# Attention and mixture-of-experts kernel: the order of TensorE's value products, scores and projection pieces within two heads

## What is computed

```python
x = x + xattn(layernorm(x), ctx)      # x: 2 x 512 x 512, ctx: 2 x 1024 x 512
x = x + ffn(layernorm(x))

# xattn: 1024 queries, 2048 keys, 16 heads of 32
q, k, v = fq_sym(q * scale), fq_sym(k), fq_sym(v)        # rounded to 255 levels
attn = softmax(einsum('bhqd,bhkd->bhqk', q, k))
attn = fq_unsigned(attn)                                 # rounded to 256 levels of the row's maximum
out = einsum('bhqk,bhkd->bhqd', attn, v) -> (1024, 512)
return out @ Wp + bp

# ffn: 8 experts; weights from x @ Wr choose the tokens' experts
h = silu(x @ Wg[e]) * (x @ Wu[e])
out = sum over e of weights[e] * (h @ Wd[e])
```

## Time and profile before

| what | value |
|---|---|
| time, median of 3 runs | 721.15 us (719.05 to 723.45) |
| the profiled execution, its own time | 722.4 us |
| its span in the trace | 720.6 us |
| TensorE busy | 617.9 us, 86% |
| VectorE busy | 567.7 us, 79% |
| ScalarE busy | 460.4 us, 64% |
| GpSimd busy | 409.7 us, 57% |
| staging of even heads (L1443) | 64 instructions, 150.2 us |
| staging halves of odd heads (L1452) | 128 instructions, 162.3 us |
| Exp (L1104) | 127 instructions, 253.2 us |

### The profile page before, as it was taken

How to read it: one execution, slowest core, us unless ns; L and a number is a source line. 1 busy time by engine, 2 the same in 40 slices (tenths; PEclk the granted TensorE clock), 3 DMA queues, 4 the chain that set the end, 5 groups by cost and what they waited for, 6 DMA issues and landing times.

```text
span 720.6 us, 16044 instructions
## 1 busy us (share of the span) xinstructions
PE 617.9 (86%) x5440; PEld 334.1 (46%) x5440; DVE 567.7 (79%) x930; ACT 460.4 (64%) x560; POOL 409.7 (57%) x457
## 2 busy tenths in 40 slices
PE   8999998666777777777768787799999999999995
PEld 4744443333534343343435355455555555555543
DVE  6998888999999999999999998793746547464430
ACT  5444459789888899898989896443534434343421
POOL 5265576655677878787877773324334453344503
PEclk9999999999999999999999997999999999999998
DMA  7877879999999999999999996258796887968724
GB/s 261 203 152 174 183 155 189 170 173 175 182 174 182 181 198 189 192 193 186 195 189 186 192 188 151 88 197 230 180 251 140 225 218 182 251 151 230 140 33 59
DMA packets 318517, 129.44 MB, mean 180 GB/s; under 512 B 293508, under 2 KB 293508, under 8 KB 318472
## 3 DMA queue, kind: packets, MB, share of 16 engines
q1 hardware_dynamic: 311296, 112.64, 72.7%
q0 software_dynamic: 7168, 16.26, 10.8%
q10 hardware_dynamic: 8, 0.01, 0.0%
HBM read 44.33 MB, written 12.06 MB: 78 GB/s over the span
## 4 chain that ended last, share of the span: by engine, by line
PE 49%; issue 11%; DMA 11%; DVE 11%; SPq 8%; ACT 5%; POOL 3%; POOLq 0%; DVEq 0%; ACTq 0%
PE psum L1724 46%; DMA work<-work 9%; DVE spare L1452 4%; ACT work L1104 4%; SPq L485 3%; SPq L483 3%; DVE spare L1443 3%; POOL work L676 1%; PE psum L1901 1%; SPq L452 1%; PE psum L2052 1%; DMA token_region<-in_L_xattn_Wkv_dram 1%; PE psum L1729 1%; POOL out_dram L858 1%; DMA work<-x_rows,slot_tok 0%
## 5 line engine op out<-in xcount | busy, mean ns | idle before, releaser
L1104 ACT ACTIVATE work<-spare,exp_bias 128x2048 uint8<-128x2048 f32 (+1 forms) x127 | 253.2, 1994 | 32.7 <-POOL exp_bias L682 21.4
L1452 DVE TENSOR_SCALAR_CACHE_REDUCE spare<-psum,q_step_now 128x1024 f32<-128x1024 f32 x128 | 162.3, 1272 | 3.4 <-PE psum L1901 3.2
L676 POOL CAST work<-work 128x2048 int16<-128x2048 uint8 x70 | 132.4, 1892 | 33.9 <-DMA work<-work 25.5
L1443 DVE TENSOR_SCALAR_CACHE_REDUCE spare<-psum,q_step_now 128x2048 f32<-128x2048 f32 x64 | 150.2, 2347 | 1.7 <-PE psum L1901 1.6
L1901 PE MATMUL psum<-keys_region,work 128*128 128x512 f16 x256 | 74.4, 395 | 42.5 <-DVE spare L1452 23.1
L846 POOL DMA_INDIRECT work<-x_rows,slot_tok x32 | 52.1, 1627 | 86.1 <-DVE slot_w L1656 72.7
L1901 PE MATMUL psum<-keys_region,bias_hl 128*128 128x512 f16 x256 | 71.0, 383 | 30.3 <-DVE spare L1452 22.9
L858 POOL DMA_INDIRECT out_dram<-keys_region,slot_tok x32 | 51.7, 1616 | 73.1 <-ACT keys_region L1199 66.1
L1860 PEld LDWEIGHTS psum<-values_region,work 128*128 128x128 f16 x2016 | 65.8, 96 | 32.1 <-POOL work L676 19.3
L1724 PE MATMUL psum<-work,spare 128*128 128x480 f16 (+1 forms) x396 | 79.4, 360 | 0.4 <-DVE work L1629 0.4
L1724 PE MATMUL psum<-work,keys_region 128*128 128x480 f16 x384 | 78.9, 366 | 0.0
(11 more groups left out here) (250 smaller groups left out, 1009.0 us busy)
## 6 DMA issues: line engine op xcount, KB each, us to landing
spare<-in_L_ffn_Wd_dram SPq DMA_DIRECT2D x8, 1024.0 KB, 15.3
spare<-in_L_ffn_Wg_dram SPq DMA_DIRECT2D x7, 1024.0 KB
spare<-in_L_ffn_Wu_dram SPq DMA_DIRECT2D x7, 1024.0 KB, 11.0
work<-in_ctx_dram SPq DMA_DIRECT2D x3, 1024.0 KB, 5.8
work<-work SPq DMA_TRANSPOSE x174, 3.7
token_region<-in_L_xattn_Wkv_dram SPq DMA_DIRECT2D x2, 1024.0 KB, 6.1
resid<-in_x_dram SPq DMA_DIRECT2D x2, 1024.0 KB, 8.8
out_dram<-work SPq DMA_DIRECT2D x8, 256.0 KB, 2.6
```

Of the source, the lines that this page charges most:

```text
L676: nc.gpsimd.tensor_copy(p_T_int[h % 4], pair_bytes[h % 4]).then_inc(unpacked, 1)
L1104: nc.scalar.activation(p_out, scores, ACT.Exp, bias=exp_bias[:, h % 4:h % 4 + 1], scale=-1.0, accum_out=p_sum[:, h:h + 1]).then_inc(exp_do ...
L1443: nc.vector.tensor_scalar(stage_home(h, first), psum[:, at:at + 4, :].rearrange("p b k -> p (b k)"), q_step_now[:, h:h + 1], None, ALU.mul ...
L1452: nc.vector.tensor_scalar(stage_home(h, first)[:, 1024 * c:1024 * c + 1024], psum[:, at:at + 2, :].rearrange("p b k -> p (b k)"), q_step_n ...
```

## The change

It touches TensorE's order in attention alone. In each group of two heads, values of head `h-6` stay ahead of the second half of head `h+1`; values of head `h-5` go behind the first half of head `h+2` and ahead of its second half. Projection pieces 0 and 1 go to the end of group `h` = 10, pieces 2 and 3 ahead of the values in group `h` = 12. In tiles 1 to 7 the throwaway matmuls of groups 10 and 12 are dropped: 2 groups by 2 matmuls by 7 tiles, 28 matmuls. No semaphore, buffer or other engine's program is changed, and values still run in the order of the heads.

```diff
-PROJECT_AT = (10, 10, 12, 12)
...
-            def after_attention(j, h):
-
-                for n, at in enumerate(PROJECT_AT):
-                    if at == h:
...
+            def project_parts(j, parts):
+
+                for n in parts:
+                    columns = slice(n * P, n * P + P)
+                    if n == 0:
+                        pe.wait_ge(wp_ready, DK)
+                    ins = project(bank(7)[:, columns], j, columns)
+                    if n == DK - 1:
+                        ins.then_inc(proj_full, 1)
...
+            def values_at(i, head, first):
+                if head >= 0:
+                    values(i, head, not first)
+                elif not first:
+                    values(i - 1, head + H, True)
+
...
-                    for head in (h - 6, h - 5):
-                        if head >= 0:
-                            values(i, head, not first)
-                        elif not first:
-                            values(i - 1, head + H, True)
-                        if head % 2 == 0 and (h or not first):
-                            throwaway(6 + head % H // HQ if head >= 0 or not first else 6, 2 if head >= 0 or not first else 8)
-                    if not first:
-                        after_attention(i - 1, h)
+                    if h == 12 and not first:
+                        project_parts(i - 1, (2, 3))
+                    values_at(i, h - 6, first)
+                    if (h or not first) and (first or h not in (10, 12)):
+                        throwaway(6 + (h + H - 6) % H // HQ if h >= 6 or not first else 6, 2 if h >= 6 or not first else 8)
                     scores(i, h + 1, 1, first)
                     if first and h == 0:
                         queries(QT - 1)
                     if h < H - 2:
-                        for n in range(2):
-                            scores(i, h + 2, n, first)
+                        scores(i, h + 2, 0, first)
+                    values_at(i, h - 5, first)
+                    if h < H - 2:
+                        scores(i, h + 2, 1, first)
+                    if h == 10 and not first:
+                        project_parts(i - 1, (0, 1))
```

More of the change, by code:

```diff
@@ L1871, in project @@
                                pieces=pieces, start=0 in pieces, stop=DK - 1 in pieces)
-            def after_attention(j, h):
-                for n, at in enumerate(PROJECT_AT):
-                    if at == h:
-                        columns = slice(n * P, n * P + P)
-                        if n == 0:
-                            pe.wait_ge(wp_ready, DK)
-                        ins = project(bank(7)[:, columns], j, columns)
-                        if n == DK - 1:
-                            ins.then_inc(proj_full, 1)
+            def project_parts(j, parts):
[6 more added lines that the diff above has]
+                        ins.then_inc(proj_full, 1)
             def scores(i, h, n, first):
```

## The result

The changed kernel takes 728.02 us (median of 6 executions, 722.89 to 732.36) against 721.88 us (6 executions, 718.37 to 723.45) for the kernel before on the same chip: a ratio of 1.0103, 95% interval 1.0072 to 1.0135. By the ratio it is slower by 1%; the medians differ by 6.1 us. The forecast of 719.0 us was wrong and its range, to 723.3, misses the time. What came is the rival with the lowest chance, TensorE's clock, at 726 us.

A forecast was written before the change was run, and what follows sets the result against it. The prediction took the loop of Exp, transpose, unpack and bias, not VectorE, to bound attention. Its terms, -2.4 us at attention's end and +0.3 us for SP, gave -2.1 us from 721.15: 719.0 us, range 715.7 to 723.3.

The forecast's parts named there:

- the rival with the lowest chance, TensorE's clock: Attention: longer TensorE gaps bring a 1.2 GHz stretch in every tile, +5 us, 726 us; chance 0.11.
- The loop bounds attention, VectorE has about 0.45 us a tile of room: Tiles 3 to 6: Exp, transpose, unpack and bias set 38.57 us a tile; VectorE alone needs 38.12.
- Projection away, values behind two more halves, covered by TensorE's idle time: TensorE in attention: moved pieces and values fit its waits; next scores at most 0.1 us late, hidden.
- VectorE's next wait, for ScalarE's Exp once a tile from tile 3 on: VectorE gets 1.3 us further ahead in tile 3, then waits for ScalarE to free its buffer.
- 0.1 us later, inside some 0.5 us of reserve: TensorE: one head's values need 0.41 us against about 0.3 us free, delaying the next scores within reserve.
- 28 throwaways dropped, worth 0 by itself: TensorE, groups 10 and 12: dropping them frees 3.4 us, all inside its waits, so no gain.
- how often the clock falls: TensorE in attention: one or two 1.2 GHz stretches in all, costing nothing but VectorE's lead.
- The case of the low clock: Attention: a 1.16 us loss in every tile puts VectorE at 39.3 us a tile, 726 us; chance 0.11.
- What VectorE's head start is worth at the end, -2.4 us: Attention's end: earlier statistics avoid the square root's collision with GpSimd's unpack; ScalarE's 2.38 us wait for `row_shift` goes.
- nothing reaches the end: Attention's end: VectorE's gain is lost, square root meets the unpack again, SP's 0.3 us stay; 721.4 us, chance 0.24.
- SP waits for later values in tile 1, +0.3 us: Tile 1: SP's transpose of head 3 waits for values ending later; bounds 0 and 2.1 us.
- the forecast's -2.1 us: Whole kernel: -2.4 us at attention's end plus 0.3 us for SP's wait, taking 721.15 to 719.0 us.

The follow-up runs named there:

- a3_full: Changed kernel with six throwaway matmuls a group in tiles 1 to 7 except group 12, and twelve or six in tile 0; ratio 1.0019 to the kernel before.
- v1_vector_plus: Kernel before with three small memsets added on VectorE at head 8 of tiles 1 to 7; ratio 1.0013.
- b0_none: Kernel before without any throwaway matmuls in tiles 1 to 7, nothing moved; ratio 1.0004.
- a2_tw_six: Changed kernel with six throwaway matmuls a group in tiles 1 to 7, none in group 12; ratio 1.0008 to the kernel before.
- w2_later_unpack: Kernel before with GpSimd's unpack of head 12 in the last tile made to wait for VectorE's `row_scaled`; median 718.62 us, ratio 0.9979.

## Why the prediction was wrong

Point by point, in its own order.

*The loop bounds attention, VectorE has about 0.45 us a tile of room.* Right. a3_full takes the waits away and its additions stay (391.62 - 237.59) / 4 = 38.51 us apart over tiles 2 to 6, inside the forecast's 38.3 to 38.6; v1_vector_plus puts VectorE's work at 38.12 us.

*Projection away, values behind two more halves, covered by TensorE's idle time.* Right at 2.4 GHz: a3_full has one wait of 0.3 us in seven tiles. Late values hold TensorE more than before there, 14.0 us against 5.5, but no longer VectorE, as the prediction had it. VectorE's next wait, for ScalarE's Exp once a tile from tile 3 on, did not appear: a3_full has none. It was the cover that failed. The prediction put the next scores "0.1 us later, inside some 0.5 us of reserve", and didn't price the same move at 1.2 GHz. There four scores take 1.52 us in place of 1.04, the values 0.48 inside the burst, and the reserve is gone. For the projection it held the 0.1 us of group 12 against the loop's room, again at full clock; behind a stretch it was up to 0.81 us.

*28 throwaways dropped, worth 0 by itself.* Within what can be measured, yes: 1.0024 (0.9989 to 1.0058) on the old order, and putting them back doesn't help the new one.

***The step that failed: how often the clock falls.*** The sum took the low clock as one or two stretches in all, which "cost nothing but VectorE's lead", and gave the other case a chance of 0.11. The runs showed nine between 113 and 430 us, in five of tiles 1 to 7, and 8.4 us of waits on VectorE (3.7 in the kernel before), which were to fall. The case of the low clock had its numbers: the longer gaps, the point of 0.45 us lost a tile, the 39.3 us a tile (GpSimd's additions came 39.3 apart), the 726 us (measured 728.0). Its gaps were a little long: 1.05 us in the plain groups where it had 1.2, against 0.66 in the kernel before and not 0.8; 1.27 in group 10 where it had 1.4; and none in group 12, where pieces 2 and 3 fill the place. Its detail was a little off: one stretch of 1.16 us in every tile, where there are 9 in seven tiles at 0.93 us each. And the price came from the earlier trace rows, the old order's tile 6, where values 0.78 us late stood ahead of the scores; b0_none shows 0.33 us as the old order's usual price. That the new order would bring a price like the dearest of the old was right by luck. The only argument against the rival was that the Trainium skill, TensorE: Matmul & The Clock Gate, section "Why this matters for your kernels", warns only of gaps much longer. The rows showed a stretch behind a gap of 0.78 us, and they should have weighed more: a change that lengthens the gap in seven of a tile's eight groups offers it seven places a tile.

*What VectorE's head start is worth at the end, -2.4 us.* The mechanism was right and the place where it ends was not. In a2_tw_six ScalarE's wait for `row_shift` is 0.18 us, as forecast, but its loop came 1.8 us later. In a3_full the loop is on time, but the square root meets the unpack at another step, and 1.86 us of waiting stay. It is the rival "nothing reaches the end": the collision is a matter of tenths. w2_later_unpack takes 1.7 us at this place by keeping the two apart, with nothing moved on TensorE.

*SP waits for later values in tile 1, +0.3 us.* Not seen. In a3_full SP issues the transpose of head 3 at 173.71 us, 0.1 us behind the values, and its residual addition of tile 2 comes at 237.59, before the 238.60 of the earlier trace rows. Within its bounds of 0 and 2.1 it is the 0.

So even at full clock the forecast's -2.1 us, a ratio of 0.997, was not there: a3_full and a2_tw_six measure 1.0019 and 1.0008, and both intervals begin above 0.997.

What stays open: why 1.05 to 1.3 us of idle time brings a stretch in one group and not in the next. The stretches fall in some tiles (three in tile 1) and spare others (none from 311 to 413 us) with the same order of work. Which group it will be is left open here, and with it any count of stretches; that they become common is what is shown.

## What to carry to other kernels

Before moving work on a fast engine into its waiting time, price the move twice, at either of the two clocks seen in the trace, and ask at which point of a burst the consumer is released. Here work ahead of a burst was free even at 1.2 GHz; the same work inside the burst, ahead of the piece that releases the consumer, ate the reserve that a low clock needs. A single stretch in the profile of before is a warning, not a singular event: a change that makes TensorE idle longer at one place of every group should be held against a kernel with the gaps filled.

## What the runs showed of the hardware

Enough thinning of TensorE's work lowered the granted clock, and enough filling of its waits raised it: without throwaways the old order had 11 stretches in place of 2, and with six a group the new one had none in place of 9. Small steps did not show: 28 throwaways fewer left the old order at 2 stretches, and 28 more left the new one at 13. From 113 to 430 us it stands at 1.00 in a3_full with TensorE busy 247.79 us, and at 0.95 in the changed kernel with 226.73 us. Busy time alone doesn't order the kernels, though: the kernel before has 234.14 us and a clock of 0.99, b0_none 233.15 us and 0.94. The useless matmuls cost nothing that could be measured where they lay in a wait.

The Trainium skill, TensorE: Matmul & The Clock Gate, section "Why this matters for your kernels", warns of idle gaps much longer than the 0.88 us and 1.05 us behind which the clock fell to 0.50 in the rows above. By it no stretch would come; the runs had up to 13 in 317 us, and the measurement decides.

A falling clock need not cost time: 11 stretches, 37.5 us at 1.2 GHz, left b0_none at 1.0004, because the engine that waits for TensorE had 0.45 us a tile to give and lost 0.53, hardly more.

A VectorE step of 0.22 us took 1.95 us beside a GpSimd cast of 1.89 us, and 0.22 again where the cast was made to wait.
